# A transformer block's front stage: scatter, zero fill and weight split moved earlier, the low half of the hidden rows subtracted by VectorE

## The reference

```python
xn = _layernorm(x)
out = x + attention(xn) + ffn(xn)
# ffn: a shared FFN over all tokens, and 16 routed experts, top 2 of a softmax router
shared = silu(xf @ Sg) * (xf @ Su) @ Sd            # Sg, Su: 256 x 256
probs = softmax(xf @ Wr); topk_p, topk_i = top_k(probs, 2)
routed = sum over e of (silu(xf @ Wg[e]) * (xf @ Wu[e]) @ Wd[e]) * cw[:, e]   # inner size 128
# attention: 16 heads of 16, block means of q and k choose per 64-token block which blocks are kept
```

## Time and profile before

| | us |
|---|---|
| median of 3 runs | 1575.19 (1572.26 to 1579.06) |
| profiled execution, its time | 1577.34 |
| its span, first to last instruction | 1575.7 |
| busy in the span: PE, DVE, ACT, POOL | 1333.9, 1047.4, 868.3, 784.8 |
| front | 0 to 305 |
| start of the experts phase up to its first expert matmul | 305.5 to 331.2 |
| 72 pairs of the experts | 331.2 to 575 |
| attention | from about 580 to the end |

### The profile page before, as it was taken

The page is one execution under the profiler, slowest core; times in us unless marked ns, Lnnn a source line. Parts: engine busy times, 40 slices in busy tenths (PEclk is TensorE's granted clock), DMA queues, the critical chain, the costliest instruction groups (busy, mean ns, idle before and its releaser), DMA issues. The chain is left out here.

```text
span 1575.7 us, 28883 instructions
## 1 busy us (share of the span) xinstructions
PE 1333.9 (85%) x8554; PEld 791.4 (50%) x8555; DVE 1047.4 (66%) x1624; ACT 868.3 (55%) x1168; POOL 784.8 (50%) x778
## 2 busy tenths in 40 slices
PE   4898884168888862799999999989999999999986
PEld 2776673168888851344444444434444444434433
DVE  5956763265555530878778888868787877877871
ACT  4444431235555530366766766666676676666664
POOL 2477878102222232157556655745754755655544
PEclk9999996579999986699999999999999999999987
DMA  5566753524444436556546547447455554654611
GB/s 183 212 235 227 250 200 124 187 88 160 148 158 151 155 111 140 200 205 221 208 164 239 195 172 249 176 157 249 177 212 192 200 216 164 248 192 159 215 36 54
DMA packets 126646, 284.67 MB, mean 181 GB/s; under 512 B 25729, under 2 KB 59649, under 8 KB 118337
## 3 DMA queue, kind: packets, MB, share of 16 engines
q1 hardware_dynamic: 108480, 230.75, 42.1%
q0 software_dynamic: 18048, 52.45, 9.5%
HBM read 152.98 MB, written 129.11 MB: 179 GB/s over the span
## 5 line engine op out<-in xcount | busy, mean ns | idle before, releaser
L1503 DVE TENSOR_REDUCE at_top<-at_ring 128x2 f32<-128x1024 f32 x512 | 621.2, 1222 | 216.5 <-PE at_ring L1637 199.1
L1463 ACT ACTIVATE at_pt<-at_ring 128x1024 f32<-128x1024 f32 x512 | 522.8, 1027 | 253.2 <-PE at_ring L1649 227.4
L1663 PE MATMUL at_ps_pv<-at_pt,at_vx 128*32 128x512 f32 x2048 | 277.7, 615 | 4.3 <-ACT at_pt L1463 4.2
L1649 PE MATMUL at_ring<-at_stack 58*128 58x512 f32 x1024 | 256.4, 498 | 21.7 <-DMA at_stack<-at_top_turned 9.5
L1637 PE MATMUL at_ring<-at_stack 56*128 56x512 f32 x1024 | 223.9, 433 | 48.0 <-DMA at_stack<-scratch_stack 28.2
L1649 PEld LDWEIGHTS at_ring<-at_stack 58*128 58x128 f32 x1024 | 96.4, 185 | 298.1 <-issue 223.6
L1355 POOL DMA_INDIRECT at_yg<-scratch_y,at_stage x128 | 125.6, 981 | 200.6 <-ACT at_pt L1463 180.0
L803 POOL DMA_DIRECT2D scratch_y<-ex_y x72 | 52.4, 728 | 218.5 <-ACT ex_y L841 214.7
L284 POOL DMA_INDIRECT scratch_xs<-fr_xn,fr_slot x128 | 126.4, 988 | 48.7 <-issue 35.9
L1637 PEld LDWEIGHTS at_ring<-at_stack 56*128 56x128 f32 x1024 | 100.1, 192 | 81.8 <-ACT at_pt L1463 37.4
L1325 POOL CAST at_qk_part<-at_qk_raw 128x512 fp32r<-128x512 f32 x64 | 39.2, 613 | 152.6 <-ACT at_qk_raw L1435 125.7
(11 more groups left out here) (203 smaller groups left out, 2426.5 us busy)
## 6 DMA issues: line engine op xcount, KB each, us to landing
at_stack<-scratch_stack SPq DMA_DIRECT2D x64, 1024.0 KB
scratch_stack<-at_qk_part SPq DMA_DIRECT2D x192, 256.0 KB, 2.5
ex_xg<-scratch_xs SPq DMA_DIRECT2D x144, 128.0 KB, 2.1
scratch_y<-ex_y POOLq DMA_DIRECT2D x72, 256.0 KB, 2.9
fr_x_in<-in_x SPq DMA_DIRECT2D x16, 512.0 KB
scratch_xp<-fr_xh SPq DMA_DIRECT2D x16, 512.0 KB
scratch_xp<-fr_xl SPq DMA_DIRECT2D x16, 512.0 KB
scratch_part<-fr_part SPq DMA_DIRECT2D x16, 512.0 KB
```

The source lines that it names most:

```text
L1463: nc.scalar.activation(pt[t][:, 2 * pair:2 * pair + 2, :], st_slot(c, j)[:], ACT.Exp, scale=float(HD) ** -0.5).then_inc(exp_ready, 1)
L1503: v.tensor_reduce(cols[:, :, TB * pair + t], slot[0][:], AX, ALU.max).then_inc(s_max, 1)
L1649: last = nc.tensor.matmul(slot[:, half, :], stack[1][r][rows, pl, t * P:(t + 1) * P], stack[0][r][rows, pl, :], start=True, stop=True)
L1663: last = nc.tensor.matmul(ps_pv[2 * HD * g:2 * HD * (g + 1), :], vx[c][:, t, G * q + g, :], pt[t][:, g, :], start=(t == 0), stop=(t == TB ...
```

## The change

In the front:
- `low_h` runs on DVE for every batch, ahead of `take_logits` (`pool_splits` returns False).
- `ranks(g)` stands on PE ahead of `down(s-1)`, and `slots(g)` on DVE in step 2g+1 (14 for the last group) instead of 2g+2; POOL scatters batch s-1 in step s.
- The expert weights are loaded within steps 0 to 11, the attention weights in step 2, and the zero fills are issued in step 15, ahead of the last two stores of `part`.
- ACT and DVE split the expert weights in the front's last steps, four experts at a time. The high parts lie where the front's `x_in`, `xh`, `xl` and four `xn` buffers are, so each piece waits until those buffers are done with.

In the experts phase the weight split and the loads are gone; the block-mean products stand ahead of pair 2; `pack` and the routing weights are spread over pairs 4 to 12 on DVE; the numbers of the experts are read after a pair's first transposes instead of ahead of them; DVE's first 16 pairs are written out instead of 4.

The core of the diff:

```diff
--- front: buffers
-        x_in = [sb(f"x_in{i}", [P, TB, D]) for i in range(2)]
-        xn = [sb(f"xn{i}", [P, TB, D]) for i in range(XN)]
+        w_at, wd_at, tile = keep["ex_w_hi_at"], keep["ex_wd_hi_at"], 4 * KD * N
+        x_in = [over(f"x_in{i}", [P, TB, D], F32, w_at + tile * i) for i in range(2)]
+        xn = [over(f"xn{i}", [P, TB, D], F32, wd_at + tile * i) for i in range(4)]
+        xn += [sb(f"xn{i}", [P, TB, D]) for i in range(4, XN)]
...
+        def pool_splits(b):
+
+            return False
+
+        CHUNK = E // 4
+        CHUNK_OF = {B - 3: 0, **{b + 1: 1 + b % XP for b in range(B - 3, B)}}
--- SyncE
+            def fill_tails():
+
+                sp.wait_ge(zero_rows, 1)
...
-                if 0 <= s < E:
-                    load_expert(s)
+                for e in range(E):
+                    if e * (B - 4) // E == s:
+                        load_expert(e)
+                if s == 2:
+                    sp.dma_start(keep["qkv_raw"][:], dram["qkv_wT"].rearrange("(k p) d -> p k d", p=P)).then_inc(at_here, 16)
+                    sp.dma_start(keep["proj_raw"][:], dram["proj_wT"].rearrange("(k p) d -> p k d", p=P)).then_inc(at_here, 16)
                 if runs(s + 2):
                     store_x(s + 2)
+                if s == B - 1:
+                    fill_tails()
                 if runs(s - 1):
                     store_part(s - 1)
--- GpSimd
-                if runs(s - 1):
+                if runs(s - 1) and pool_splits(s - 1):
                     low_h(s - 1)
                 if runs(s + 4):
                     root(s + 4)
-                if s < B - 1 and runs(s - 2):
-                    scatter(s - 2)
-                elif s == B - 1:
-                    scatter(B - 3)
-                    scatter(B - 2)
-            scatter(B - 1)
+                if runs(s - 1):
+                    scatter(s - 1)
--- ScalarE
+            def high_w(c, b):
+
+                act.wait_ge(ex_here[c], 48 * CHUNK)
+                if c == 0:
+
+                    act.wait_ge(xn_ready, B)
+                else:
+                    act.wait_ge(gu_in_psum, b + 1)
+                    act.wait_ge(x_stored[b % XP], 32 * (b // XP + 1))
...
+            def high_wd(c):
+
+                for i in range(4):
+                    act.wait_ge(scattered[i], 16 * 2 * TB * (B // XN))
...
+                if s in CHUNK_OF:
+                    high_w(CHUNK_OF[s], s - 1)
+                if s == B - 1:
+                    for c in range(2):
+                        high_wd(CHUNK_OF[B - 3 + c])
+                if s == B:
+                    for c in range(2):
+                        high_wd(CHUNK_OF[B - 1 + c])
--- VectorE
+            def low_h(b):
+                dve.wait_ge(hh_ready, b + 1)
+                if b >= 2:
+
+                    dve.wait_ge(out_in_psum, 2 * (b - 1))
+                v.tensor_tensor(hl[b % 2][:], hid[:], f32(hh[b % 2][:]), ALU.subtract).then_inc(hl_ready, 1)
...
+                if runs(s - 1) and not pool_splits(s - 1):
+                    low_h(s - 1)
...
-                if s >= 2 and s % 2 == 0 and s // 2 - 1 < GROUPS - 1:
-                    slots(s // 2 - 1)
-                if s == B - 1:
-                    slots(GROUPS - 1)
-                    list_tiles()
+                for g in range(GROUPS):
+                    if count_step(g) == s:
+                        slots(g)
+                if s == B - 2:
+                    v.tensor_copy(zero_row[:], ps_count[0:1]).then_inc(zero_rows, 1)
...
+                if s == B - 2:
+                    list_tiles()
+                    low_w(CHUNK_OF[B - 3], 0)
+                if s == B - 1:
+                    low_w(CHUNK_OF[B - 2], 1)
             take_list()
...
+            low_w(CHUNK_OF[B - 1], 2)
+            for n in range(4):
+                low_wd(CHUNK_OF[B - 3 + n], n)
+            low_w(CHUNK_OF[B], 3)
--- TensorE: ranks(g) is taken from behind down(s - 1, 1) and put ahead of down(s - 1, 0)
+                        pe.wait_ge(l_ready, min(s + 2, B))
+                        ranks(g)
--- experts phase: TensorE
             def step(p, i):
                 inside = not isinstance(p, int) or p < PAIRS
-                experts = experts_of(p)
                 if inside:
                     transpose_x(p, i)
+                experts = experts_of(p)
...
+                if p == 2:
+                    pe.wait_ge(sums_ready, 1)
...
--- experts phase: VectorE
+                if 5 <= p < 11:
+                    pack((p - 5) // 3, (p - 5) % 3)
+                if p == 11:
+                    dve.wait_ge(exp_ready, 1)
+                    done(v.tensor_reduce(total[:], by_e[1][:], AX, ALU.add))
```

More of the change, by code:

```diff
@@ L96, in phase_front @@
         minus_half = sb("minus_half", [P, TB])
-        xh = [sb(f"xh{i}", [P, KD, N], F32R) for i in range(XP)]
-        xl = [sb(f"xl{i}", [P, KD, N], F32R) for i in range(XP)]
+        xh = [over(f"xh{i}", [P, KD, N], F32R, w_at + tile * (2 + 2 * i)) for i in range(XP)]
+        xl = [over(f"xl{i}", [P, KD, N], F32R, w_at + tile * (3 + 2 * i)) for i in range(XP)]
         w_part = [sb(f"w_part{x}", [P, KD, 2, FS], F32R) for x in range(2)]
@@ L109, in phase_front @@
         logitT = sb("logitT", [E, N])
-        logit = sb("logit", [P, NT, E])
-        top = [sb(f"top{j}", [P, NT]) for j in range(2)]
+        logit, top, slot_f, gap, edge = keep["logit"], keep["top"], keep["slot_f"], keep["gap"], keep["edge"]
         equal, cand, rest = (sb(n, [P, G2, E]) for n in ("equal", "cand", "rest"))
@@ L124, in phase_front @@
         zeros = sb("zeros", [P, D])
-        small = {name: sb(name, [P, E]) for name in ("count", "tiles", "end", "gap", "last_one", "edge")}
+        small = {name: sb(name, [P, E]) for name in ("count", "tiles", "end", "last_one")}
         count_i, tiles_i = sb("count_i", [P, E], I32), sb("tiles_i", [P, E], I32)
@@ L145, in phase_front @@
         w_here, w_high, w_low = sem("w_here"), sem("w_high"), sem("w_low")
-        ex_here, ex_high = sem("ex_here"), sem("ex_high")
+        ex_here = [sem(f"ex_here{c}") for c in range(4)]
+        ex_high, exd_high, at_here = sem("ex_high"), sem("exd_high"), sem("at_here")
         x_here = [sem(f"x_here{i}") for i in range(2)]
@@ L498, in list_tiles @@
                 order.done(v.tensor_reduce(cols[:, 0, :], ended[:], AX, ALU.add))
[L499 removed]
+                do(v.tensor_tensor(skipped[:], ended[:], gap[:].unsqueeze(1).broadcast_to([P, JC, E]), ALU.mult))
                 do(v.tensor_reduce(offset[:], skipped[:], AX, ALU.add))
@@ L654, in _ @@
                     list_rows()
+                for g in range(GROUPS):
+                    if count_step(g) == s:
+                        pe.wait_ge(l_ready, min(s + 2, B))
+                        ranks(g)
+                        if g == GROUPS - 1:
+                            nc.tensor.matmul(ps_count, ones[:], carry[GROUPS % 2][:], start=True,
+                                             stop=True).then_inc(count_in_psum, 1)
                 if runs(s - 1):
@@ L660, in _ @@
                     down(s - 1, 1)
-                for g in range(GROUPS):
-                    if count_step(g) == s:
-                        if runs(s + 2):
-                            pe.wait_ge(lT_ready, s + 3)
-                        ranks(g)
-                        if g == GROUPS - 1:
-                            nc.tensor.matmul(ps_count, ones[:], carry[GROUPS % 2][:], start=True,
-                                             stop=True).then_inc(count_in_psum, 1)
                 if runs(s + 2):
@@ L811, in _ @@
         def _(act):
-            for c in range(CHUNKS):
-                experts = slice(c * WC, (c + 1) * WC)
-                nc.scalar.copy(w_part[0][:, experts].rearrange("p e k f -> p (e k f)"),
-                               keep["ex_w_raw"][:, experts].rearrange("p e k f -> p (e k f)"))
-                nc.scalar.copy(wd_part[0][:, experts], keep["ex_wd_raw"][:, experts]).then_inc(w_high, 1)
             def step(p, i):
```

165 lines of the change are left out of this document (85 added, 80 removed).

## The result

The changed kernel took 1528.28 us (median of 4 runs, 1525.98 to 1532.54), the kernel before beside it 1576.43: a ratio of 0.970, interval 0.967 to 0.973. Forecast were 1503, with a range up to 1526. The kernel is faster, by 48 us and not by 72. So the first thing to know of the missing 24 us is that they don't belong to the program alone.

What follows compares the result with a forecast made beforehand. GpSimd was taken to set the front's pace, PE close behind. Front -57.0, experts' start -16.7, pair loop +4.0, +3.0 and -5.0 make -71.7 us against 1577.34: 1505.6, as shown median 1503; range 1485 to 1526.

Steps and rivals of the forecast that it cites:

- First batch to last scatter: Front: GpSimd's scatters start at 55.0 and the last call ends at 245.7 instead of 281.9, about 12.0 us a step.
- the waits for slots: Front: GpSimd, at 11.4 us a step against PE's 11.7, waits now and then for slots: 4 us (0 to 8).
- The last calls of the phase: End of the front: only the last scatter's landing, 2 to 3 us, is late; the experts phase starts at 248.5.
- VectorE's wait for the cast: Front: `low_h` on VectorE waits for ACT's cast, which is released early enough; priced at nothing.
- The lock: Front: VectorE's subtractions stretch GpSimd's scatter calls: 5.6 us for `low_h` (0 to 10.5), 4.6 for the weight split (0 to 8.5).
- the second rival: Front: VectorE's `low_h` and the split hold GpSimd for their whole time, 30.8 us instead of 10.2: 1524; chance 0.10.
- Zero fills: End of the front: 18.2 us of issue, ending at about 226 and landing at 234, hidden under the scatter.
- The start: Start of the experts phase, before its first expert matmul: 9.0 us instead of 25.7, a gain of 16.7.
- rival 4: Front: VectorE blocked in order, `low_h` waiting for ACT's cast; at 7 us of wait 18.1 a step, 1594; chance 0.02.
- rival 5: Front: the DMA engines set the pace; held at 255 GB/s the step is 13.9 us, total 1530; chance 0.04.
- The pair loop: Experts phase: block-mean products +4.0, `pack` and weights on VectorE +3.0, experts' numbers read after the transposes -5.0 us.
- Rival 1: Front: engines passing work in order can't be full; at 13 us a step, 14 steps cost 14 more: 1517; chance 0.21.

Runs made afterwards that it cites:

- run 5: The changed kernel unaltered, measured again on the second chip: 1496.16 us, 0.951 of the kernel before.
- run 3: The kernel before with only `low_h` moved from GpSimd to VectorE: 1588.29 us, 1.003 of the kernel before.
- run 10: The changed kernel unaltered, measured again on the third chip: 1526.69 us, 0.963 of the kernel before.
- run 1: The changed kernel with a small GpSimd power ahead of every 4 scatter calls from batch 10 on: 1523.82 us, 0.963 of the kernel before.
- run 2: The changed kernel with `low_h` on GpSimd again for all batches: 1542.47 us, 0.976 of the kernel before.
- run 6: The changed kernel with one GpSimd power ahead of each batch's 8 scatter calls from batch 10 on, second chip: 1501.96 us, 0.952 of the kernel before.
- run 7: The changed kernel with GpSimd waiting, from batch 10 on, until the batch before has landed, second chip: 1511.67 us, 0.960 of the kernel before.
- run 8: The changed kernel with the experts' numbers read ahead of a pair's transposes again: 1506.77 us, 0.958 of the kernel before.
- run 11: The changed kernel with one GpSimd power ahead of each batch's scatters from batch 10 on, third chip: 1511.98 us, 0.952 of the kernel before.
- run 12: The changed kernel with GpSimd waiting, from batch 10 on, until the batch before has landed, third chip: 1523.46 us, 0.961 of the kernel before.

## Why the prediction was wrong

Point by point, in the prediction's order.

- **First batch to last scatter.** First scatter: 54.20 and 51.4 in two traces, 55.0 forecast. Last call over at 258.6, 12.9 late. By terms, from the first call on: the calls and the gaps between them without anything beside them 159.1 us (162.2 forecast), stretched by VectorE 7.9 (128 calls of 1.022 instead of 0.96 us; 10.2 forecast; 13.8 in run 5), `root` and its gaps 13.6 (14.3). **The term that failed is the waits for slots: 4 (0 to 8) forecast, 23.8 in 6 waits measured**, in run 5 1.4. The step of about 12.0 us was 12.4 and, where nothing was late, 11.7; in the kernel before it was 14.5 on average (eight steps from 76.89 to 192.59) and not always the 13.72 of the one that the prediction shows.
- **The last calls of the phase.** "What is late next is the last scatter's landing, 2 to 3 us": 22.7 us instead, **the second term that failed**. ScalarE's last copy stood at 270.7. Behind it came VectorE's splits until 278.6 and SP's store of the copy, the last of all:

```profile
SPq L246 <- DMA scratch_part<-fr_part: 6.4, 1, 6.4
```

SP waited until 280.70 for the landing, and the phase began at 281.30. 12.9 and 19.9 make the 32.8. I had added up GpSimd's work and left PE's results to arrive in time. In run 5, where nothing was late, it was 7.3 us, so this term was too small there as well: the last scatter landed 1.4 us after the end of its call, and then GpSimd's own drain at the phase's end took 5.3 (241.38 to 246.67). In the first trace the drain lay within the wait.
- **VectorE's wait for the cast**, "priced at nothing": VectorE stood 19.9 us in 5 waits ahead of `low_h`, the longest 9.4, each behind ScalarE's cast; in run 5 2.2. It is the same delay passed on, since the cast queues behind the late copies.
- **The lock.** The scatter call at 231.92 took 2.73 us: the weight subtraction beside it (231.53, 2.29 us) still had 1.90 to go, and the call was 1.77 longer than 0.96. Most calls that began inside such a subtraction show the same, the rest of it less 0.12 us; calls that had begun before it kept their 0.96. So the 0.96 beside the operation at 155.56, on which the forecast rested its lower end, was read wrongly: that call had begun 0.04 us earlier and says nothing of one that begins later. Over all calls it was cheap because few begin inside one, and the second rival is refuted as a price; that its 1524 lies near the result is luck.
- **Zero fills** were not hidden under the scatter in the first trace: their issue ran from 239.24 to 270.51, 12 us past the last call, and the last two stores of `part` stood behind it. It took 31.27 us against 18.56 in run 5 and 18.2 forecast; why is open. With VectorE busy until 278.6 it can have cost 2 us at most. **The start** of the experts phase: 8.15, forecast 9.0. **Ordering of VectorE's queue** as slower than before (rival 4) and **the DMA engines** (rival 5: shares of 0.77 to 0.79 with 275 to 285 GB/s in a step): refuted.
- **The pair loop.** Forecast +2.0; three traces of the changed kernel say -2.7, +0.7 and -0.6, the kernel before itself varies by 1.8 between two. The read was worth 3.1 where it was undone.
- **Rival 1**, that engines passing work in order would make the step 13 us and the time 1517, was nearest in kind. It named the place, `slots` waiting for PE, but not the mechanism, and the loss isn't spread over 14 steps: the first nine (64.49 to 176.03) kept 12.4 us. Two of the prediction's own signs of being wrong came: `low_h` waiting for ScalarE, and the phase starting after 262.

The reason is the one hidden in "GpSimd's own work can't end before 231.5": taking `low_h` from GpSimd, and having no `root` after step 11, took away the pauses in which PE's increments came through. I read "PE idle <- GpSimd's `low_h`" as the whole of the coupling. The kernel before had 51 us (29.6 and 21.6) of ScalarE's waits for "remote" in front of operations that wait for PE, and the working gives them no cause. The Trainium skill (Perfetto Trace Analysis, section Tensor Engine Instruction (MATMUL, LD_WEIGHTS)) says that a matmul's end in the profile is computed and that its semaphore is updated only once PSUM acknowledges the write; the trace agrees as far as it goes. In run 5 the gap between the profiled end and the recorded increment was never over 0.3 us; in the first trace it reached 15.8 us, for which that section has no reason.

Shown: the late increments, that they shrink when GpSimd is made to pause in the tail, their absence in all four kernels on one of the three chips, their price (1526.69 and 1528.28 against 1496.16 for one program, of which up to 8.5 us are also between the kernels before; 15 us got back by six powers). Not shown: whether GpSimd's issue or the scatters' traffic holds the increments, what in the chip does it, why one chip doesn't, and whether it is the chip, the place of the core on it or the time of the runs.

## What to carry to other kernels

Where GpSimd issues many indirect DMAs, look at the first operation behind each PE result: if it starts microseconds after the matmul's end and its wait is called "remote" with no DMA among its conditions, GpSimd's scatters may be on PE's path, and work taken off GpSimd can lengthen it. A pause of a microsecond every eight calls gave 15 of some 30 us back here, and cost 6 us where nothing was late (within the intervals). When a front is to end with GpSimd's last scatter, count its drain too. And a gain of a few per cent wants measuring on more than one chip.

## What the runs showed of the hardware

- In the first two traces and on two of the three chips of the later runs, many of TensorE's recorded semaphore increments that fell into a run of GpSimd's indirect DMAs (0.96 us each, 0.30 apart) came over 0.3 us late: 38 of 67 in the changed kernel's first trace, up to 15.8 us (18.9 in run 3). In that first trace those that came after the end of the run came 0.8 to 2.4 us after it. On one chip, with four programs, none was late. No recorded increment of VectorE, ScalarE or GpSimd was late in any of them.
- The delays are regular: ScalarE's longest waits in the tail were 11.35 and 18.94 us in the first trace and 11.40 and 18.77 in that of run 10.
- A scatter call that began inside a VectorE subtraction with both inputs in SBUF was longer by what was left of it less 0.12 us (1.77 at 231.92; 2.09 at 217.11 in run 5, beside 2.29); one that had begun before it stayed at 0.96. VectorE was not slowed.
- Wherever GpSimd was the last engine of the front, the next phase began 7.2 to 7.3 us after the end of its last scatter call (runs 1, 2, 5 to 8, 11 and 12), 5.3 of it GpSimd's drain.
